# Two orders changed: when the down weights and the next block's x are handled in the first feed-forward block, and which bank holds two rounds' attention values

## What is computed

```python
x = layernorm(x + attention(x))        # q = x Wq (semantic and rotary), pooled keys, softmax, values, Wo
x = layernorm(x + ffn(x))

def ffn(x):                            # x: 4096 x 512
    x = fwht(x * SU_ug) / 64
    up, gate = x @ W_up.T * s_up, x @ W_gate.T * s_gate      # 2048 each
    h = fwht(silu(gate) * up * SU_dp) / 64
    return h @ W_down.T * s_dp
```

## Time and profile before

| | |
|---|---|
| times of three runs | 1573.79 us median, 1571.07 to 1574.36 |
| the profiled execution | 1574.06 us, of which the span is 1572.3 us |
| busy shares of the span | PE 97%, weight loads 87%, DVE 66%, ACT 40%, POOL 30% |
| attention | 0 to 530 us, four batches |
| first feed-forward block | 530 to 675 us |
| the seven other blocks | 126.9 us each |

### The profile page before, as it was taken

One profiled execution on the slowest core, in us unless ns is written; L12 is line 12 of the kernel. 1 busy time (PEld: TensorE's weight loads), 2 busy tenths in 40 slices (PEclk: granted clock), 3 DMA queues, 4 the chain that ended last, 5 costly groups with the idle time before them and its releaser, 6 DMA issues.

```text
span 1572.3 us, 26383 instructions
## 1 busy us (share of the span) xinstructions
PE 1526.9 (97%) x10152; PEld 1369.7 (87%) x10152; DVE 1035.4 (66%) x1790; ACT 626.3 (40%) x1289; POOL 467.0 (30%) x580
## 2 busy tenths in 40 slices
PE   6999999999998999999999999999999999999998
PEld 5977977887787888899999999999999999999997
DVE  6876776676687877875575575566466557557545
ACT  4154245236226745533333343343343333333332
POOL 5465456447338533600120030030040021003001
PEclk9999999999999999999999999999999999999999
DMA  7031022122112786588668677767776857766862
GB/s 280 1 105 77 34 82 100 35 81 101 63 62 101 268 335 258 210 296 299 224 229 293 221 249 247 275 206 261 267 242 222 309 201 251 279 235 220 276 233 94
DMA packets 92059, 307.42 MB, mean 196 GB/s; under 512 B 9888, under 2 KB 10272, under 8 KB 90144
## 3 DMA queue, kind: packets, MB, share of 16 engines
q1 hardware_dynamic: 90928, 301.54, 54.2%
q10 hardware_dynamic: 1008, 4.20, 0.7%
HBM read 255.37 MB, written 50.33 MB: 194 GB/s over the span
## 4 chain that ended last, share of the span: by engine, by line
PE 62%; DVE 6%; ACT 1%; issue 1%; POOL 0%; DVEq 0%; POOLq 0%; ACTq 0%
PE ff_bank_b L2009 16%; PE ff_bank_c L2009 10%; PE ff_bank_a L2009 10%; PE ff_acc L107 7%; PE ff_acc L109 7%; PE ff_acc L108 7%; DVE ff_d_lo L1723 2%; DVE ff_ring L1718 1%; PE ff_x_ps L1960 1%; PE ff_x_ps L1980 1%; ACT at_union L589 1%; DVE ff_c L1774 0%; PE ff_x_ps L1968 0%; PE ff_x_ps L1969 0%; DVE ff_c L1770 0%
## 5 line engine op out<-in xcount | busy, mean ns | idle before, releaser
L2009 PE MATMUL ff_bank_b<-ff_x_hi,ff_ring 128*128 128x256 f32 x1536 | 302.8, 280 | 4.7 <-DVE ff_c L1774 4.3
L2009 PEld LDWEIGHTS ff_bank_b<-ff_x_hi,ff_ring 128*128 128x128 f32 x1536 | 247.9, 188 | 6.5 <-issue 6.2
L2009 PE MATMUL ff_bank_b<-ff_x_lo,ff_ring 128*128 128x256 f32 x768 | 214.3, 279 | 0.0
L2009 PE MATMUL ff_bank_c<-ff_x_hi,ff_ring 128*128 128x256 f32 x1024 | 205.4, 283 | 1.2 <-DVE ff_ring L1718 1.0
L2009 PE MATMUL ff_bank_a<-ff_x_hi,ff_ring 128*128 128x256 f32 x1024 | 203.5, 282 | 0.0
L107 PE MATMUL ff_acc<-ff_d_hi,ff_h_hi 128*128 128x512 f32 x504 | 200.8, 399 | 1.7 <-DVE ff_d_lo L1723 1.7
L109 PE MATMUL ff_acc<-ff_d_hi,ff_h_lo 128*128 128x512 f32 x504 | 196.6, 390 | 0.0
L108 PE MATMUL ff_acc<-ff_d_lo,ff_h_hi 128*128 128x512 f32 x504 | 196.3, 389 | 0.0
L2009 PEld LDWEIGHTS ff_bank_c<-ff_x_hi,ff_ring 128*128 128x128 f32 x1024 | 166.1, 189 | 4.0 <-issue 2.1
L2009 PEld LDWEIGHTS ff_bank_a<-ff_x_hi,ff_ring 128*128 128x128 f32 x1024 | 165.3, 188 | 2.7 <-issue 0.2
L1770 DVE TENSOR_TENSOR ff_c<-ff_bank_b,ff_c 128x512 f32<-128x512 f32 x64 | 44.2, 691 | 180.1 <-PE ff_bank_b L2009 179.2
(11 more groups left out here) (315 smaller groups left out, 3480.7 us busy)
## 6 DMA issues: line engine op xcount, KB each, us to landing
ff_ring<-gu_scratch SPq DMA_DIRECT2D x392, 512.0 KB, 5.0
gu_scratch<-ff_ring SPq DMA_DIRECT2D x56, 512.0 KB, 4.1
at_xt<-in_xt SPq DMA_DIRECT2D x4, 2048.0 KB, 8.0
at_xn<-in_x SPq DMA_DIRECT2D x32, 256.0 KB, 2.9
x_scratch<-at_x SPq DMA_DIRECT2D x32, 256.0 KB, 2.0
ff_raw<-in_wgu SPq DMA_DIRECT2D x8, 1024.0 KB, 6.6
at_wd_a<-in_wd SPq DMA_DIRECT2D x8, 512.0 KB, 4.7
mixed_scratch<-at_wd_a SPq DMA_DIRECT2D x8, 512.0 KB, 3.3
```

What stands on the lines that cost most here:

```text
L2009: i = pe.matmul(bank[:, m, :], r[:, a, m, c, :], b[:, k, c, :], start=(k < 3 and m == 0 and c == 0 and b is x_hi and a == 0), stop=(m == 1 ...
```

## The change

Attention, in all four batches: the values of groups 0 and 5 go to bank `acc` instead of `tr` (`value_bank`), so PE's waits for a free bank change; ACT and DVE read group 0 and group 4 out one round later (rounds 3 and 7, behind the split of the turned probabilities), instead of in rounds 2 and 6. DVE adds tile 5's residual in round 2 instead of round 1, and its statistics behind that round's reciprocals. POOL's inverse deviation of tile 5 moves behind the normalisation of pair 7 (from pair 4), ACT's scaling of tiles 4 and 5 to the front part of rounds 4 and 5 (from the end of rounds 3 and 4). PE multiplies group 0's values before it turns the queries.

First feed-forward block: ACT and DVE do `split_down` as the first thing of a step, in steps 1 to 7. The eight operations on the next block's x move from steps 4 to 6 to steps 3 to 5 (`FIRST_X_AT`). In step 0 ACT writes the first folded chunk back one operation earlier. The other blocks are as they were.

```diff
@@ -274,6 +274,10 @@
+        def value_bank(i):
+            return acc if i in (0, 5) else tr
@@ -463,8 +467,8 @@
                             rotate_local(b, 1, 1)
-                        if tt == 0 and p in (3, 4):
-                            inverse_deviation(b, RT - 5 + p)
+                        if tt == 0 and p in (3, 7):
+                            inverse_deviation(b, RT - 2 + p // 7)
                         if tt and p == 5:
@@ -609,6 +613,15 @@
+                def outputs_hi(i):
+                    tt, g = divmod(i, HKV)
+                    act.wait_ge(*pv_ps.now(b, BLOCKS[i][-1] + 1))
+                    if tt == 1:
+                        act.wait_ge(*out_ps.now(b, RT + 1))
+                    for r, c, n, at in output_rows(tt, g):
+                        k = act.activation(qo_hi[r, c:c + n, :].rearrange("p j q -> p (j q)"), value_bank(i)[r, at:at + P * n], ACT.Copy)
+                    k.then_inc(o_hi_s.sem, 1)
@@ -616,6 +629,10 @@
                             act.activation(tp_hi[:, n % 2, :], mid[:, n % 2, :], ACT.Copy).then_inc(tp_hi_s.sem, 1)
+                    if i in (3, 7):
+                        outputs_hi(i - 3)
+                    if i in (4, 5):
+                        scale_x1(b, RT - 6 + i)
                     if i == 3:
@@ -630,18 +647,10 @@
                         local_exponentials(i)
-                    if i >= 2:
-                        tt, g = divmod(i - 2, HKV)
-                        act.wait_ge(*pv_ps.now(b, BLOCKS[i - 2][-1] + 1))
-                        if tt == 1:
-                            act.wait_ge(*out_ps.now(b, RT + 1))
-                        for r, c, n, at in output_rows(tt, g):
-                            k = act.activation(qo_hi[r, c:c + n, :].rearrange("p j q -> p (j q)"), tr[r, at:at + P * n], ACT.Copy)
-                        k.then_inc(o_hi_s.sem, 1)
+                    if i >= 2 and i not in (2, 6):
+                        outputs_hi(i - 2)
                     if not more and 4 <= i <= GROUPS:
                         ahead.first_products(i)
-                    if i in (3, 4):
-                        scale_x1(b, RT - 5 + i)
                     if i == 7:
@@ -882,11 +891,27 @@
                         residual(b, t - 2)
+                def outputs_lo(i):
+                    tt, g = divmod(i, HKV)
+                    dve.wait_ge(*o_hi_s.now(b, i + 1))
+                    for r, c, n, at in output_rows(tt, g):
+                        v = lambda q: q[r, c:c + n, :].rearrange("p j q -> p (j q)")
+                        k = dve.tensor_tensor(v(qo_lo), value_bank(i)[r, at:at + P * n], v(qo_hi).bitcast(F32), ALU.subtract)
+                    k.then_inc(o_lo_s.sem, 1)
+                def reciprocals(i):
+                    tt, g = divmod(i, HKV)
+                    for p in (2 * g, 2 * g + 1):
+                        dve.wait_ge(*lexp.now(b, 8 * tt + p + 1))
+                        dve.reciprocal(stat[:, tt, 3, 2 * p:2 * p + 2], stat[:, tt, 1, 2 * p:2 * p + 2]).then_inc(lrecip.sem, 1)
...
                             dve.tensor_tensor(tp_lo[:, n % 2, :], mid[:, n % 2, :], tp_hi[:, n % 2, :].bitcast(F32), ALU.subtract).then_inc(tp_lo_s.sem, 1)
+                    if i in (3, 7):
+                        outputs_lo(i - 3)
                     if not more and i == 9:
@@ -900,7 +925,6 @@
                     if i < GROUPS:
-                        tt, g = divmod(i, HKV)
                         if i == 3:
@@ -909,20 +933,15 @@
                             residual(b, RT - 2)
-                        for p in (2 * g, 2 * g + 1):
-                            dve.wait_ge(*lexp.now(b, 8 * tt + p + 1))
-                            dve.reciprocal(stat[:, tt, 3, 2 * p:2 * p + 2], stat[:, tt, 1, 2 * p:2 * p + 2]).then_inc(lrecip.sem, 1)
-                        if i == 1:
-                            residual(b, RT - 1)
+                        if i == 2:
+                            add_residual(b, RT - 1)
+                        reciprocals(i)
+                        if i == 2:
+                            add_statistics(b, RT - 1)
                     if i == 6:
                         residual(b, TILES - 2)
-                    if i >= 2:
-                        tt, g = divmod(i - 2, HKV)
-                        dve.wait_ge(*o_hi_s.now(b, i - 1))
-                        for r, c, n, at in output_rows(tt, g):
-                            v = lambda q: q[r, c:c + n, :].rearrange("p j q -> p (j q)")
-                            k = dve.tensor_tensor(v(qo_lo), tr[r, at:at + P * n], v(qo_hi).bitcast(F32), ALU.subtract)
-                        k.then_inc(o_lo_s.sem, 1)
+                    if i >= 2 and i not in (2, 6):
+                        outputs_lo(i - 2)
                     if not more and 4 <= i <= GROUPS:
@@ -1196,11 +1215,12 @@
-                    pe.wait_ge(*(o_lo_s.now(b, i) if i else added.now(b, RT)))
+                    pe.wait_ge(*(added.now(b, RT - 1) if i == 0 else added.now(b, RT) if i == 1 else added.now(b, RT + 1) if i == 5 else
+                                 o_lo_s.now(b, 5 if i == 6 else i)))
                     w = slice(P * (g // 2), P * (g // 2) + P)
...
                         pe.wait_ge(*tp_lo_s.now(b, n + 1))
-                        three_passes(pe, tr[:, :], v_hi[:, k, w], v_lo[:, k, w], tp_hi[:, n % 2, :], tp_lo[:, n % 2, :],
+                        three_passes(pe, value_bank(i)[:, :], v_hi[:, k, w], v_lo[:, k, w], tp_hi[:, n % 2, :], tp_lo[:, n % 2, :],
                                      k == 0, n == BLOCKS[i][-1]).then_inc(pv_ps.sem, 1)
@@ -1214,8 +1234,6 @@
                         attend_pooled(b, RT - 1, True, True).then_inc(out_ps.sem, 1)
-                    if i == 2:
-                        transpose_queries(b, 1)
                     if i == 6:
@@ -1234,6 +1252,8 @@
                         local_values(i - 2)
+                    if i == 2:
+                        transpose_queries(b, 1)
                 output(b, TILES - 1, 1)
@@ -1347,8 +1367,13 @@
+        FIRST_X_AT = {(3, 3): ("turn", 0), (3, 6): ("mix", 0), (3, 8): ("turn", 1), (4, 3): ("mix", 1), (4, 6): ("turn", 2),
+                      (4, 8): ("mix", 2), (5, 3): ("turn", 3), (5, 6): ("mix", 3)}
         X_AT = {(4, 3): ("turn", 0), (4, 6): ("mix", 0), (4, 8): ("turn", 1), (5, 3): ("mix", 1), (5, 6): ("turn", 2),
...
+        def x_at(blk):
+            return X_AT if blk else FIRST_X_AT
@@ -1593,6 +1618,8 @@
                 produce = lambda k: round_product(MULS * p + k + AHEAD) if first and MULS * p + k + AHEAD < PRODUCTS else None
+                if first and not opening:
+                    split_down(s, p - 1, first)
                 act.wait_ge(*mul_s.now(s, 1))
@@ -1602,7 +1629,7 @@
                     first_x(5)
-                else:
+                elif not first:
                     split_down(s, (p - 1) % PAIRS, first)
@@ -1623,10 +1650,10 @@
                 produce(4)
+                if opening:
+                    fold_down(0)
                 act.wait_ge(*evict_s.now(s, 4))
                 silu(p, 1, c2[:, :, 0, :], by_half(sg[:, 1, :])).then_inc(silu_s.sem, 1)
-                if opening:
-                    fold_down(0)
                 if first:
@@ -1651,8 +1678,8 @@
             def at(act, blk, p, pos, last):
-                if not last and (p, pos) in X_AT:
-                    what, c = X_AT[p, pos]
+                if not last and (p, pos) in x_at(blk):
+                    what, c = x_at(blk)[p, pos]
                     (split_turned if what == "turn" else keep_mixed)(blk + 1, c)
@@ -1828,15 +1855,15 @@
+                if not opening:
+                    split_down(s, p - 1)
                 evict_m6(s)
...
                     split_x(0, 5)
-                elif closing:
-                    split_down(s, p - 1)
-                else:
+                elif not closing:
                     lower_h(s - 1)
@@ -2034,14 +2059,14 @@
                     folded = 0 if not first else 2 * p + (pos > 1) + (pos > 7)
-                    if not last and (p, pos) in X_AT:
-                        what, c = X_AT[p, pos]
+                    if not last and (p, pos) in x_at(blk):
+                        what, c = x_at(blk)[p, pos]
                         if what == "turn":
...
                     if first and pos in fold_at(p):
-                        done = [X_AT[at][0] for at in X_AT if at < (p, pos)]
+                        done = [FIRST_X_AT[at][0] for at in FIRST_X_AT if at < (p, pos)]
                         mix_down(2 * p + pos // 7, done.count("turn"), done.count("mix"))
```

## The result

Over 21 runs of each kernel on one chip the changed kernel takes 1577.24 us (median; 1573.03 to 1579.85), the kernel before 1573.53 us (1570.98 to 1576.32). The ratio is 1.002 with a 95% interval of 1.0013 to 1.0026. The profiled execution took 1577.54 us with a span of 1575.7, against 1574.06 and 1572.3 before, so the two profiles differ by about as much as the medians (3.4 us against 3.7) and the loss can be looked for in them. It is a loss clear of noise, outside my range (1567.5 to 1572.8) and outside the one given for 8 in 10 (1563.5 to 1574.3).

What follows compares the result with a forecast made beforehand. PE, busy 1526.9 of 1572.3 us, was taken as the bound. From 1574.06: -4.5 (rounds), +1.6 (step 1), -1.1 (step 2), -0.4 (step 3), +0.4 (steps 6 and 7), in sum -4.0, gave 1570.1 us; range 1567.5 to 1572.8.

Steps and rivals of the forecast that it cites:

- the gain of the rounds: Attention, all four batches: shorter PE waits win 1.15 us a batch, 1.05 in the last, 4.5 us together.
- the clock behind step 1's waits: First feed-forward block, step 1: the clock falling as in step 7 costs 1.2 us, counted only in the bounds.
- The readings of rounds 2 and 3: Attention: POOL's normalising limits round 2 to 0.2 us; the queries' low half leaves 0.45 of round 3's 1.3 us.
- round 5's wait: Attention, round 5: PE's wait of 0.57 us for `tp_lo` goes, 0.7 us with the restart.
- The last batch: Attention, last batch: extra work for the first block leaves a piece of the waits, so 1.05 us won.
- Step 1: First feed-forward block: ACT comes late to the split at the head, 1.6 us lost; bounds 1.0 won to 2.8 lost.
- Steps 2 and 3: First feed-forward block: the down product no longer waits, winning 1.1 us in step 2 and 0.4 in step 3.
- Steps 6 and 7: First feed-forward block: POOL slows DVE, PE waits 2.9 to 3.9 us at k = 3; 0.4 us lost overall.
- no sum: First feed-forward block: moving the x operations from step 6 to step 3 neither wins nor loses time.
- Rival (c): Whole kernel slower, 1579.6 us: low clock behind step 7's wait, block loses 7.3, rounds win only 1.8; chance 0.06.
- Rival (b): Rounds give nothing, POOL's pairs or the queries' low half taking freed waits; block loses 0.5: 1574.5 us; chance 0.12.
- (a): Block gains too, DVE catching up at the heads of steps 1 and 7: 1564.8 down to 1560.5 us; chance 0.20.

Runs made afterwards that it cites:

- e2_block_alone: The kernel before with only the change's feed-forward part, attention as before: 1576.23 us, ratio 1.0014 to the kernel before.
- e3_scales_early: The changed kernel with DVE's two small scalings moved ahead of round 4's reciprocals in the last batch: 1574.80 us, ratio 1.0006 to the kernel before.
- e9_x_old: The changed kernel with the second block's x operations back in steps 4 to 6, splits still at the heads: 1573.73 us, ratio 1.0002 to the kernel before.

## Why the prediction was wrong

I forecast 1570.1 and gave slower a chance of 0.06; the ratio says slower by 0.2%. Two steps failed: the gain of the rounds, -4.5 us in the sum, which the runs show as +0.6, and the clock behind step 1's waits, which I had left to the bounds.

- **Rounds, -4.5 forecast, +0.6 found** (from 0.26 ahead to 0.34 behind). The readings of rounds 2 and 3 were right in kind: POOL's normalising holds round 2 (pair 3 is done at 228.27, PE turns it at 228.32), the queries' low half takes round 3's gain back (PE's wait for it is 1.09, foreseen about 0.9), round 5's wait goes. The sizes were not. Of the 1.15 us a batch, batch 1 won 0.64 within its rounds: 0.18 up to the output product (0.45 forecast), which is round 2's alone, as the low half takes back all of round 3's, 0.58 at round 5's values (0.7 forecast), less 0.11 at round 6's scores, whose wait grew from 0.27 to 0.38 where I had it shrink to 0.05. Another 0.24 went between the last round and the next batch, in a stretch in which PE has no wait in either trace (50.19 against 50.43 us). It is for the most part the query projection (0.116 us a matmul against 0.120), and since e2_block_alone has the slower pace with the old code, it is not the change; why PE has two paces there is open. Batches 0 to 2 won 1.3 us together where 3.45 were forecast, 1.9 without this.
- **The last batch.** Forecast at -1.05, it lost 1.9 against the profile before: a step that the sum didn't have. With the collision taken out (e3_scales_early) it loses 0.26 and the time is 2.2 us less. The old order can run into it too (e2_block_alone), so how much of it is owed to the change in the 21 runs is open. I said of the last batch only that extra work leaves a piece of the waits (1.05 for 1.15), and did not ask which POOL work the two scalings would now meet. The rows were there: POOL's butterfly starts 0.01 us after DVE's second scaling in the trace of before. The Trainium skill ("SBUF — State Buffer", section "Who interferes with whom") says that `tensor_scalar` in its two-port mode contends with GpSimd as well as operations with two SBUF inputs do, and that the issue order decides who blocks; the 0.88 us of the first scaling, which has one SBUF input, agree with it. I had used that rule for d_lo alone.
- **Step 1, +1.6 forecast, +3.3 found.** The chain to the first wait was right to 0.4 us, and k = 5 came 0.2 us behind the forecast, although `h_lo` took 3.45 us and not 2.39. What failed is the clock behind the two waits: the twelve matmuls of k = 5 took 2.62 us in the changed kernel and 1.49 in e2_block_alone, where the clock stayed up and steps 0 and 1 lost 1.4. It was in the bounds, not in the sum.
- **Steps 2 and 3, -1.5 forecast, -1.1 found.** Step 2 won 0.6 of its 1.1, as a new wait of 0.46 stands at its k = 5; step 3, 18.37 us less 1.2 for its three new x operations, won the 0.4.
- **Steps 6 and 7, +0.4 forecast, +0.9 found.** The wait of 2.9 to 3.9 at k = 3 came as 3.62, and the clock fell as assumed. The step was right: from step 6's start to the next block 39.52 us, at the far end of the 38.5 to 39.5 forecast. What I had wrong is the share of the edits: I put the loss on the split at the head, and the runs put as much on the early x operations, which I had called "no sum" (e9_x_old); either one undone gives back 2.8 us by the ratios.
- **Rival (c)** was on the right side with the wrong bound: it needed 7.6 us lost in the block because it left the rounds their gain. The block lost 3.1, and the rounds lost 0.6. Of its mechanism the loss in step 1 came, the long fall of the clock in step 7 did not (0.92 over the step, as before). Rival (b) had the rounds right in kind (the freed waits taken by the queries' low half, no gain in sum) and the block too small, 0.5 lost. (a) is out: step 7 has a wait of 3.62 us.

## What to carry to other kernels

When an edit moves one engine's list against another's, list every operation that will now meet the other engine's work, the small ones too: a 0.16 us operation that meets a 1.3 us one costs 1.3, and whatever is queued behind it pays. When a wait is removed, look at what stands directly behind in the same queue and who wants it next; here the read-out that was moved ahead of the queries' low half ate the gain, and behind it the gain came through. Price a stall on PE of about 2 us with the clock that may fall behind it. And before a loss is put down to the new order, look whether the old order escapes it by a hair: here by 0.01 us.
